# Where SBUF buffers start: weights on multiples of 2048 bytes, TensorE's activations and the other large buffers 256 bytes past one, on one Trainium2 core

## The chip, the core and the metric

The kernel runs on one core of a Trainium2 chip. Its time is the device time of one execution in microseconds (us); each version is run several times, and the median counts. The engines are TensorE (PE), VectorE (DVE), ScalarE (ACT), GpSimd (POOL) and SyncE (SP), which issues the transfers. A profiled execution of the kernel before gives the trace that is read below.

## The reference

One transformer-like layer in fp32 over B=4 sequences of T=2048 tokens with D=512 channels, modulated by a small matrix (`wmod`):

```python
mod = (silu(c) @ wmod).reshape(4, 6, 1, -1)
sa, ca, ga, sb, cb, gb = (mod[:, i] for i in range(6))
# ga and gb keep their sign and are at least 0.25 in size
h = layernorm(x) * (1 + ca) + sa
x = x + ga * attn(h)
h = layernorm(x) * (1 + cb) + sb
x = x + gb * ffn(h)

# attn: per token omega, zeta and B from h (three projections, 256 columns in all), a scan over
# time of a 2 x 64 state, then xs @ C.T + h @ D_mat.T
# ffn: xr, xk are mixes of a token with the one before it;
#      sigmoid(xr @ Wr.T) * (square(relu(xk @ Wk.T)) @ Wv.T)
```

## The kernel before

Work goes by *chunks* of 512 tokens (16, index q) for the first norm, the projections and the scan, and by *units* of 256 tokens (32, index u) for the rest. P=128 partitions, KC=4 slices of the 512 channels. Every engine has its own instruction stream, written out by hand as a loop over the units; semaphores (`s_...`) tie them together. Nothing else sets the order.

Each matrix product is made in three passes from a high and a low half in fp32r (`_hi`, `_lo`): hi*hi, hi*lo and lo*hi, four slices each. `product()` issues them as `pe.matmul(out, act[a][k], weight[w][k])`. The second argument is loaded into the array (the *stationary* tile, an LDWEIGHTS of 128 columns, 512 bytes a partition), the third streams through it (*moving*). One load goes with each matmul. In every unit PE does:

- `k_product`: `wk` stationary, `mix_k` (256 columns) moving, 48 matmuls into `ps_kr`
- `t2_blocks`: 8 transposes with `xn2` stationary and `ident` moving
- `cd_product`: 24 matmuls with `h` stationary and a row of `wd` (512 columns, 2048 bytes) moving, then `states_part`, 6 with `xs` stationary and `wc` moving, into `ps_cd`
- `r_product`: 24 with `mix_r` stationary and `wr` moving, 512 columns, into `ps_kr`
- `v_product`: 24 with `kk` stationary and `wv` moving, 512 columns, into `ps_tv`
- in every second unit `projections`, 24 with `proj` stationary and `h` moving, 512 columns, and 16 transposes of `x_in` (stationary)

All of these but the transposes carry line 328 (`product`) in the trace, so they are told apart by their tiles, out<-in.

Buffers are placed one behind the other in the order of their declaration by `sb(...)`, from byte 1152 of each partition on. So a buffer's address follows from the sizes of those ahead of it. The remainders of the start address, in bytes (every slice that is used adds a multiple of 512):

| buffer | role on PE | past a multiple of 2048, before | past a multiple of 128, before | past a multiple of 2048, after |
|---|---|---|---|---|
| `proj`, `wk` | stationary | 1152 | 0 | 0 |
| `wd`, `wc`, `wr`, `wv` | moving | 1152 | 0 | 0 |
| `h` (both pairs) | stationary, moving in the projections | 384 | 0 | 256 |
| `mix_k` | moving | 576 | 64 | 256 |
| `mix_r`, `kk_hi`, `kk_lo` | stationary | 576 | 64 | 256 |
| `xs_hi`, `xs_lo` | stationary | 2016 | 96 | 256 |
| `xn2` | stationary | 576 | 64 | 256 |
| `x_in` | stationary | 1728 | 64 | 256 |
| `ident` | moving | 1152 | 0 | 256 |
| `x2`, `h_full` | none | 384 | 0 | 256 |
| `rt`, `kk`, `mix_full` | none | 576 | 64 | 256 |
| `xs` | none | 2016 | 96 | 256 |
| `gate_a`, `gate_b` | none | 1696 | 32 | 256 |
| `square_out1` | none | 352 | 96 | 256 |
| `om_pos`, `ze`, `ee` | none | 576 | 64 | 1728 |

Before, the buffers end at byte 229344; after, at 228428.

The second norm (LN2) of a unit runs over several engines: DVE multiplies the product in `ps_cd` by the gate into `xn2` (`rt` for unit 1) and adds it to `x2` with a sum; ACT makes the mean and then, in `statistics2`, the squares with their sum; POOL makes the reciprocal root; DVE writes the normalised unit into `xn2` (`normalise2`), which PE transposes. ACT's squares are wanted for their sums alone; where the squares themselves go, nobody reads.

Of the kernel before, what the change touches and what calls it, by code (L numbers as in the profile page):

```python
# [7 lines left out]
F32 = mybir.dt.float32  # L8
F32R = mybir.dt.float32r
# [3 lines left out]
B, T, D, M = 4, 2048, 512, 64  # L13
P = 128
# [24 lines left out]
def build(nc, d):  # L39
    ctx = ExitStack()  # L40
    with ctx:
# [5 lines left out]


        proj = [sb(f"proj_{n}", [P, KC, 256], F32R) for n in ("hi", "lo")]
        wd = [sb(f"wd_{n}", [P, KC, D], F32R) for n in ("hi", "lo")]  # L50
        wc = [sb(f"wc_{n}", [P, D], F32R) for n in ("hi", "lo")]
        wk = [sb(f"wk_{n}", [P, KC, D], F32R) for n in ("hi", "lo")]
        wr = [sb(f"wr_{n}", [P, KC, D], F32R) for n in ("hi", "lo")]
        wv = [sb(f"wv_{n}", [P, KC, D], F32R) for n in ("hi", "lo")]
        ident = sb("ident", [P, P])
        scan_bias = sb("scan_bias", [P, 4])
# [10 lines left out]
        cur_m = sb("cur_m", [P, NTAB])  # L67
        gate_a = sb("gate_a", [P, D])
        gate_b = sb("gate_b", [P, D])
        minus_half = sb("minus_half", [P, TPC])  # L70

        x_in = sb("x_in", [P, TPC, D])
        gate_cols = sb("gate_cols", [P, 3, 2, B * D // P])
# [6 lines left out]
        bn = sb("bn", [P, TPC, 2])  # L80
        square_out1 = sb("square_out1", [P, 2, D], mybir.dt.bfloat16)
        square_out2 = sb("square_out2", [P, 2, D], mybir.dt.bfloat16)
        rstd1 = sb("rstd1", [P, TPC])
        h_full = sb("h_full", [P, KC, CHUNK])
        h = [[sb(f"h_{n}{i}", [P, KC, CHUNK], F32R) for n in ("hi", "lo")] for i in range(2)]

        x2 = sb("x2", [P, 4, TPU, D])
        sum2 = sb("sum2", [P, 2, TPU])
# [4 lines left out]
        last_n = sb("last_n", [P, KC])  # L93
        mix_full = sb("mix_full", [P, 2, KC, UNIT])
        mix = [mix_full[:, n] for n in range(2)]


        with nc.sbuf_tensor("stage_mix", [P, 2, KC, D], F32) as stage_mix:
            pass
        mixs = [[sb(f"mix_{n}_{w}", [P, KC, UNIT], F32R) for w in ("hi", "lo")] for n in "kr"]  # L100
        with nc.sbuf_tensor("stage_kk", [P, KC, D], F32) as stage_kk:
            pass
        kks = [sb(f"kk_{m}", [P, KC, UNIT], F32R) for m in ("hi", "lo")]
        with nc.sbuf_tensor("stage_out", [P, KC, D], F32) as stage_out:
            pass
        xn2 = sb("xn2", [P, TPU, D])
        rt = sb("rt", [P, TPU, D])
        kk = sb("kk", [P, 2, 2 * UNIT])

        om_pos = sb("om_pos", [P, HALF])  # L110
# [9 lines left out]
        state = sb("state", [P, 3, HALF + 1])  # L120
        xs = sb("xs", [P, CHUNK])
        xss = [sb(f"xs_{m}", [P, CHUNK], F32R) for m in ("hi", "lo")]

# [444 lines left out]
        def _(act):  # L568
# [8 lines left out]
            def squares(x, neg_mean, scratch, out, count, s_sq):  # L577

                for i in range(out.shape[1]):
                    if count + i >= 2:  # L580
                        act.wait_ge(s_sq, count + i - 1)
                    act.activation(scratch[:, i % 2, :], x[:, i, :], ACT.Square, bias=neg_mean[:, i:i + 1],  # L582
                                   accum_out=out[:, i:i + 1]).then_inc(s_sq, 1)
# [5 lines left out]
            def statistics2(u):  # L589
                act.wait_ge(s_x2, u * TPU + TPU)  # L590
                act.activation(neg_mean2[:, u % 2, :], sum2[:, u % 2, :], ACT.Identity, scale=-1.0 / D)\
                   .then_inc(s_mean2, 1)
                act.wait_ge(s_mean2, u + 1)
                squares(x2[:, u % 4], neg_mean2[:, u % 2], square_out2, sq2[:, u % 2], u * TPU, s_sq2)

# [959 lines left out]
```

## Time and profile before

| | |
|---|---|
| median of 3 timed runs | 976.72 us (976.17 to 977.73) |
| the profiled execution, its time | 977.14 us |
| its span in the trace, first to last instruction | 975.4 us |
| busy: PE, DVE, ACT, POOL | 935.9, 820.9, 691.5, 93.5 us |
| mean granted TensorE clock | 0.981 |

A group's "mean ns of one" is the length of one record. Matmuls overlap in it, so the pace of PE is read from the starts: the start of one group of a timeline minus the start of an earlier one, divided by the matmuls between. The granted clock is a share of 2.4 GHz; 0.50 is 1.2 GHz.

### The profile page before, as it was taken

Reading aid. Unit: us, or ns where it says so; the run is one execution under the profiler, and the core shown is the slowest. Engines: PE = TensorE matmul, PEld = TensorE weight load, DVE = VectorE, ACT = ScalarE, POOL = GpSimd, SP = SyncE. Lnnn points to the kernel's source line nnn. Section 1 sums busy time; section 2 is a strip of 40 time slices with the busy share of each in tenths; the row PEclk is TensorE's granted clock in tenths of the full one; section 3 lists DMA queues with packets and bytes.
Section 4 is the critical chain, followed back from the end, with each engine's and each line's share of the span. In section 5 each row is a group of like instructions: output and inputs, shape, how many; then the busy total and the mean of one; then the engine's idle time right before and its main releaser. Section 6 shows DMA issues by size and latency. Waiting matters only on the chain.

```text
span 975.4 us, 14746 instructions
## 1 busy us (share of the span) xinstructions
PE 935.9 (96%) x5012; PEld 786.9 (81%) x5012; DVE 820.9 (84%) x2280; ACT 691.5 (71%) x1354; POOL 93.5 (10%) x117
## 2 busy tenths in 40 slices
PE   9995979899999999999999999999999999998997
PEld 3574858788888888888888888888888888887886
DVE  4897779898989989898998979898997989697562
ACT  4979765768777686777868686877768677765451
POOL 0001010001100202010200101110110201000000
PEclk9997998999999999999999999999999999999999
DMA  9820311020211312021121312021131201111001
GB/s 327 280 56 23 109 34 53 12 98 23 87 55 44 99 44 70 18 87 44 57 85 44 98 32 77 23 87 45 44 98 44 98 6 39 44 44 44 23 22 44
DMA packets 35275, 64.78 MB, mean 66 GB/s; under 512 B 3704, under 2 KB 4344, under 8 KB 35200
## 3 DMA queue, kind: packets, MB, share of 16 engines
q1 hardware_dynamic: 35200, 63.84, 19.8%
q8 instruction: 40, 0.66, 0.3%
q14 instruction: 35, 0.29, 0.1%
HBM read 47.02 MB, written 16.81 MB: 65 GB/s over the span
## 4 chain that ended last, share of the span: by engine, by line
PE 83%; DVE 8%; ACT 6%; issue 1%; DMA 1%; DVEq 0%; SPq 0%; ACTq 0%
PE ps_kr L328 32%; PE ps_cd L328 20%; PE ps_tv L328 18%; PE ps_pt L328 7%; PE ps_tv L369 3%; PE ps_pt L336 3%; ACT mix_full L734 1%; DMA stage_out<-in_wd 1%; DVE mix_full L985 1%; PE ps_cd L376 1%; DVE tmp L1206 1%; ACT x_in L600 1%; DVE state L1210 1%; PE ps_tv L389 0%; DVE tmp L1130 0%
## 5 line engine op out<-in xcount | busy, mean ns | idle before, releaser
L985 DVE SCALAR_TENSOR_TENSOR mix_full<-ps_tv,cur_m,mix_full 128x256 f32<-128x256 f32 x256 | 119.1, 479 | 37.7 <-ACT mix_full L734 37.6
L756 ACT ACTIVATE kk<-ps_kr 128x512 f32<-128x512 f32 x64 | 38.1, 599 | 123.4 <-PE ps_kr L328 123.1
L734 ACT ACTIVATE mix_full<-ps_tv,cur_m 128x255 f32<-128x255 f32 x256 | 120.0, 573 | 1.8 <-PE ps_tv L369 1.8
L1484 POOL TENSOR_SCALAR var<-sq 128x2 f32<-128x2 f32 (+1 forms) x34 | 37.1, 1091 | 642.5 <-ACT square_out L582 642.5
L328 PE MATMUL ps_kr<-mix_k_hi,wk_hi 128*128 128x256 f32 x512 | 80.9, 281 | 8.2 <-issue 8.2
L328 PEld LDWEIGHTS ps_kr<-mix_k_hi,wk_hi 128*128 128x128 f32 x512 | 71.2, 191 | 11.2 <-issue 8.8
L328 PE MATMUL ps_kr<-mix_k_hi,wk_lo 128*128 128x256 f32 x512 | 80.1, 279 | 0.0
L328 PE MATMUL ps_kr<-mix_k_lo,wk_hi 128*128 128x256 f32 x512 | 80.0, 279 | 0.0
L328 PE MATMUL ps_kr<-wr_hi,mix_r_hi 128*128 128x512 f32 x256 | 71.5, 402 | 5.5 <-ACT kk L756 5.5
L328 PE MATMUL ps_tv<-wv_hi,kk_hi 128*128 128x512 f32 x256 | 72.8, 408 | 0.8 <-issue 0.8
L328 PE MATMUL ps_kr<-wr_hi,mix_r_lo 128*128 128x512 f32 x256 | 69.9, 395 | 0.0
L328 PE MATMUL ps_tv<-wv_lo,kk_hi 128*128 128x512 f32 x256 | 69.9, 395 | 0.0
L328 PE MATMUL ps_kr<-wr_lo,mix_r_hi 128*128 128x512 f32 x256 | 69.8, 395 | 0.0
L328 PE MATMUL ps_tv<-wv_hi,kk_lo 128*128 128x512 f32 x256 | 69.1, 392 | 0.0
L328 PEld LDWEIGHTS ps_kr<-mix_k_lo,wk_hi 128*128 128x128 f32 x512 | 69.0, 190 | 0.0
L328 PEld LDWEIGHTS ps_kr<-mix_k_hi,wk_lo 128*128 128x128 f32 x512 | 68.6, 190 | 0.0
L328 PE MATMUL ps_cd<-wd_hi,h_hi 128*128 128x512 f32 x248 | 68.1, 396 | 0.0
L328 PE MATMUL ps_cd<-wd_lo,h_hi 128*128 128x512 f32 x248 | 66.4, 390 | 0.0
L328 PE MATMUL ps_cd<-wd_hi,h_lo 128*128 128x512 f32 x248 | 66.4, 389 | 0.0
L748 ACT ACTIVATE mix_k_hi<-mix_full 128x512 fp32r<-128x512 f32 x64 | 40.4, 641 | 33.9 <-DVE mix_full L985 33.6
L328 PEld LDWEIGHTS ps_kr<-wr_hi,mix_r_hi 128*128 128x128 f32 x256 | 47.6, 191 | 15.7 <-issue 5.9
L328 PEld LDWEIGHTS ps_tv<-wv_lo,kk_hi 128*128 128x128 f32 x256 | 49.1, 192 | 11.3
(213 smaller groups left out, 2239.6 us busy)
## 6 DMA issues: line engine op xcount, KB each, us to landing
x<-in_x SPq DMA_DIRECT2D x32, 512.0 KB, 3.7
out<-x SPq DMA_DIRECT2D x32, 512.0 KB, 2.8
x_in<-in_x SPq DMA_DIRECT2D x15, 1024.0 KB, 5.1
x<-in_wmod SPq DMA_DIRECT2D x3, 1024.0 KB, 7.6
mix_full<-in_wmod SPq DMA_DIRECT2D x2, 1024.0 KB, 9.1
x_in<-in_x SPq DMA_DIRECT2D x2, 512.0 KB, 5.7
stage_out<-in_wd SPq DMA_DIRECT2D x1, 1024.0 KB, 10.0
stage_mix<-in_wmod SPq DMA_DIRECT2D x1, 1024.0 KB, 10.5
```

Of the source, the lines that this page charges most:

```text
L328: mm = pe.matmul(out, act[a][k], weight[w][k], start=acc0 and a == 0 and w == 0 and k == 0, stop=acc1 and (a, w) == passes[2] and k == n - 1)
L336: mm = pe.transpose(ps_pt[:, k % 2, i * P:(i + 1) * P], x_in[:, i, k * P:(k + 1) * P], ident[:, :])
L369: mm = pe.transpose(ps_tv[:, k // 2, at:at + P], xn2[:, i, k * P:(k + 1) * P], ident[:, :])
L376: pe.matmul(bank, warm[:, 0:P], warm[:, :], start=True, stop=True)
L600: mm = act.activation(x_in[:, i, :], x_in[:, i, :], ACT.Identity, bias=norm_bias1[:, i:i + 1], scale=rstd1[:, i:i + 1])
L734: mm = act.activation(mix[n][:, k, 1:UNIT], ps_tv[:, j, c * UNIT:(c + 1) * UNIT - 1], ACT.Identity, bias=cur_m[:, SHIFT + k:SHIFT + k + 1] ...
L748: act.activation(mixs[n][0][:, 2 * j:2 * j + 2, :], mix[n][:, 2 * j:2 * j + 2, :], ACT.Identity)\
L756: act.activation(kk[:, i, :], ps_kr[:, i, :], ACT.Relu).then_inc(s_relu, 1)
L985: dve.scalar_tensor_tensor(mix[n][:, k, :], ps_tv[:, j, c * UNIT:(c + 1) * UNIT], cur_m[:, alpha + k:alpha + k + 1], mix[n][:, k, :], ALU. ...
L1206: dve.tensor_tensor(t, node, frm.unsqueeze(1).broadcast_to([P, 2, 3, c]), ALU.mult)\
L1210: dve.tensor_reduce(to[:, 0:2], t.rearrange("p i j c -> p i c j"), mybir.AxisListType.X, ALU.add)\
L1484: pool.tensor_scalar(var[:, :], sq[:, :], 1.0 / D, EPS, ALU.mult, ALU.add).then_inc(s_var, 1)
```

## The change

Two unused buffers push the next ones to chosen addresses: `to_2048` (896 bytes) puts `proj` at byte 2048, and since all weights have a multiple of 2048 bytes, the others follow on such multiples; `by_256` (256 bytes) puts everything after it 256 bytes past one. The declarations of the large buffers that are read or written by PE, ACT and DVE come next, all multiples of 2048 bytes long, and the small ones behind them. To make room, `square_out2` is dropped, a bf16 buffer of 2048 bytes for LN2's squares. They now go to `xn2` (to `rt` in unit 1), in fp32, and the two waits of the squares on earlier squares are left out there. No engine's instructions change in number or place.

```diff
+        sb("to_2048", [P, 224])
         proj = [sb(f"proj_{n}", [P, KC, 256], F32R) for n in ("hi", "lo")]
         wd = [sb(f"wd_{n}", [P, KC, D], F32R) for n in ("hi", "lo")]
         wc = [sb(f"wc_{n}", [P, D], F32R) for n in ("hi", "lo")]
         wk = [sb(f"wk_{n}", [P, KC, D], F32R) for n in ("hi", "lo")]
         wr = [sb(f"wr_{n}", [P, KC, D], F32R) for n in ("hi", "lo")]
         wv = [sb(f"wv_{n}", [P, KC, D], F32R) for n in ("hi", "lo")]
+        sb("by_256", [P, 64])
+        h = [[sb(f"h_{n}{i}", [P, KC, CHUNK], F32R) for n in ("hi", "lo")] for i in range(2)]
+        xss = [sb(f"xs_{m}", [P, CHUNK], F32R) for m in ("hi", "lo")]
+
+        with nc.sbuf_tensor("stage_mix", [P, 2, KC, D], F32) as stage_mix:
+            pass
+        mixs = [[sb(f"mix_{n}_{w}", [P, KC, UNIT], F32R) for w in ("hi", "lo")] for n in "kr"]
+        with nc.sbuf_tensor("stage_kk", [P, KC, D], F32) as stage_kk:
+            pass
+        kks = [sb(f"kk_{m}", [P, KC, UNIT], F32R) for m in ("hi", "lo")]
+        with nc.sbuf_tensor("stage_out", [P, KC, D], F32) as stage_out:
+            pass
+        xn2 = sb("xn2", [P, TPU, D])
+        rt = sb("rt", [P, TPU, D])
+        kk = sb("kk", [P, 2, 2 * UNIT])
+        x_in = sb("x_in", [P, TPC, D])
+        h_full = sb("h_full", [P, KC, CHUNK])
+        x2 = sb("x2", [P, 4, TPU, D])
+        mix_full = sb("mix_full", [P, 2, KC, UNIT])
+        mix = [mix_full[:, n] for n in range(2)]
+        xs = sb("xs", [P, CHUNK])
+        gate_a = sb("gate_a", [P, D])
+        gate_b = sb("gate_b", [P, D])
+        square_out1 = sb("square_out1", [P, 2, D], mybir.dt.bfloat16)
+
         ident = sb("ident", [P, P])
...
-        square_out2 = sb("square_out2", [P, 2, D], mybir.dt.bfloat16)
...
                 for i in range(out.shape[1]):
-                    if count + i >= 2:
+                    if scratch is square_out1 and count + i >= 2:
                         act.wait_ge(s_sq, count + i - 1)
                     act.activation(scratch[:, i % 2, :], x[:, i, :], ACT.Square, bias=neg_mean[:, i:i + 1],
...
-                squares(x2[:, u % 4], neg_mean2[:, u % 2], square_out2, sq2[:, u % 2], u * TPU, s_sq2)
+
+                squares(x2[:, u % 4], neg_mean2[:, u % 2], rt if u == 1 else xn2, sq2[:, u % 2], u * TPU, s_sq2)
```

The lines that the diff takes out elsewhere are the same declarations at their old places.

## Rows read from the trace of the kernel before

**Rows 1.** The page's head: span, busy us of each engine.
```profile
span 975.4 us, 14746 instructions
PE 935.9 (96%) x5012; PEld 786.9 (81%) x5012; DVE 820.9 (84%) x2280; ACT 691.5 (71%) x1354; POOL 93.5 (10%) x117
```

**Rows 2.** Windows: stretch, its length, busy us of each engine (instructions), clock, DMA.
```profile
400.00:600.00 200.00, 200.00 (x1107) 172.87 (x1106) 177.53 (x501) 153.38 (x300) 23.27 (x25) 1.00 0.19 60
600.00:800.00 200.00, 200.00 (x1106) 173.05 (x1105) 179.73 (x504) 149.69 (x296) 23.49 (x26) 1.00 0.17 57
```

**Rows 3.** Waits from 200 to 900 us: us in total, times, longest.
```profile
ACT kk L756 <- PE ps_kr L328: 93.9, 40, 4.9
```

**Rows 4.** Timeline of PE, 446 to 476 us: start us, us, group.
```profile
447.35 1.08 PE L328 MATMUL ps_kr<-wr_lo,mix_r_hi 128*128 128x512 f32 x4
...
451.92 1.07 PE L328 MATMUL ps_cd<-wd_hi,h_hi 128*128 128x512 f32 x4
...
453.74 1.07 PE L328 MATMUL ps_cd<-wd_hi,h_lo 128*128 128x512 f32 x4
...
457.37 0.39 PE L328 MATMUL ps_cd<-wc_hi,xs_hi 128*128 128x512 f32 x1
...
458.77 1.08 PE L328 MATMUL ps_tv<-wv_hi,kk_hi 128*128 128x512 f32 x4
459.69 1.08 PE L328 MATMUL ps_tv<-wv_lo,kk_hi 128*128 128x512 f32 x4
...
464.27 0.64 PE L328 MATMUL ps_kr<-mix_k_hi,wk_hi 128*128 128x256 f32 x4
...
465.66 0.62 PE L328 MATMUL ps_kr<-mix_k_hi,wk_hi 128*128 128x256 f32 x4
...
469.74 1.04 PE L369 MATMUL ps_tv<-ident,xn 128*128 128x128 f32 x8
470.53 1.17 PE L328 MATMUL ps_cd<-wd_hi,h_hi 128*128 128x512 f32 x4
```

**Rows 5.** The same, from 439.9 to 446.6 us.
```profile
442.80 1.07 PE L328 MATMUL ps_pt<-h_hi,proj_lo 128*128 128x512 f32 x4
...
446.43 0.39 PE L328 MATMUL ps_kr<-wr_hi,mix_r_hi 128*128 128x512 f32 x1
```

**Rows 6.** Groups by form: count, busy us, mean ns of one, idle before.
```profile
L328 PE MATMUL ps_kr<-wr_hi,mix_r_lo 128*128 128x512 f32 x256 | 69.9, 395 | 0.0
...
L328 PE MATMUL ps_cd<-wd_hi,h_lo 128*128 128x512 f32 x248 | 66.4, 389 | 0.0
...
L328 PE MATMUL ps_cd<-wc_hi,xs_lo 128*128 128x512 f32 x62 | 25.6, 412 | 0.0
```

**Rows 7.** By tile: count, duration in ns min/median/max, first and last start.
```profile
L582 ACT ACTIVATE square_out<-x,neg_mean x64: 705/717/726, 57.1 to 925.9; 128x512 bf16<-128x512 f32 x64
...
L770 ACT ACTIVATE kk_hi<-kk x64: 617/657/689, 90.7 to 960.2; 128x512 fp32r<-128x512 f32 x64
```

**Rows 8.** Near the end: timeline of PE, and a window's clock.
```profile
900.10 0.77 PE L328 MATMUL ps_cd<-wc_hi,xs_hi 128*128 128x512 f32 x1 [4.24 <-DVE xs_lo L916]
...
909.79 0.64 PE L328 MATMUL ps_kr<-mix_k_lo,wk_hi 128*128 128x256 f32 x4
...
914.50 0.64 PE L328 MATMUL ps_kr<-mix_k_hi,wk_lo 128*128 128x256 f32 x4
...
898.20:905.00 6.80, 4.90 (x12) 3.87 (x13) 5.61 (x11) 2.96 (x7) 0.00 (x0) 0.50 0.00 0
```

**Rows 9.** The chain's first 30 us; transfers: count, KB, us to landing.
```profile
12.77 9.96 DMA stage_out<-in_wd
...
x<-in_wmod SPq DMA_DIRECT2D x3, 1024.0 KB, 7.6
mix_full<-in_wmod SPq DMA_DIRECT2D x2, 1024.0 KB, 9.1
```

**Rows 10.** Windows 200 to 976 us: PE reading `wr_hi`, then `wc_hi` (counts).
```profile
200.00:976.00 776.00, 121.93 (x464) 0.99 0.17 54
...
200.00:976.00 776.00, 38.08 (x104) 0.99 0.17 54
```

More of the change, by code:

```diff
@@ L67, in build @@
         cur_m = sb("cur_m", [P, NTAB])
-        gate_a = sb("gate_a", [P, D])
-        gate_b = sb("gate_b", [P, D])
         minus_half = sb("minus_half", [P, TPC])
-        x_in = sb("x_in", [P, TPC, D])
         gate_cols = sb("gate_cols", [P, 3, 2, B * D // P])
@@ L80, in build @@
         bn = sb("bn", [P, TPC, 2])
-        square_out1 = sb("square_out1", [P, 2, D], mybir.dt.bfloat16)
-        square_out2 = sb("square_out2", [P, 2, D], mybir.dt.bfloat16)
         rstd1 = sb("rstd1", [P, TPC])
-        h_full = sb("h_full", [P, KC, CHUNK])
-        h = [[sb(f"h_{n}{i}", [P, KC, CHUNK], F32R) for n in ("hi", "lo")] for i in range(2)]
-        x2 = sb("x2", [P, 4, TPU, D])
         sum2 = sb("sum2", [P, 2, TPU])
@@ L93, in build @@
         last_n = sb("last_n", [P, KC])
[L94 to L108, printed above, removed]
         om_pos = sb("om_pos", [P, HALF])
@@ L120, in build @@
         state = sb("state", [P, 3, HALF + 1])
-        xs = sb("xs", [P, CHUNK])
-        xss = [sb(f"xs_{m}", [P, CHUNK], F32R) for m in ("hi", "lo")]
         x2_a, x2_b = (x2[:, i:i + 2].rearrange("p a t n -> p (a t) n") for i in (0, 2))
```

## The prediction

> **What bounds the kernel now.** I read the page's head first: TensorE is busy for 935.9 of 975.4 us [rows 1]. A share says nothing of who waits, so the windows came next: from 400 to 800 us PE is busy for 200.00 of 200 us twice (the stretch from 200 us on reads alike), while VectorE (DVE) has 177.5 of 200 and ScalarE (ACT) 153.4 of 200 [rows 2]. The longest wait that the sums name between other engines and PE is ACT's for PE, 93.9 us [rows 3]. So every nanosecond by which a matmul follows its forerunner sooner is kept, as long as DVE, with a tenth of the time free, does not come into the way. Before 200 us the chain runs through ACT, DVE and a 9.96 us landing of `wd` [rows 9], and near the end PE waits once, for 4.24 us, for `xs_lo` [rows 8].
>
> Then I read how fast PE goes, from the starts of its groups in one unit in the bound stretch [rows 4]. All products with 512 columns have the same shape, and their pace differs:
> - `wd` products (4 matmuls a row): from 453.74 to 457.37 us are 16 matmuls, 226.9 ns each. The projections from 442.80 to 446.43 us [rows 5]: 226.9 ns also.
> - `wr` products: 447.35 to 451.92 us, 20 matmuls, 228.5 ns. `wv`: 459.69 to 464.27 us, 20 matmuls, 229.0 ns. Together 9.15 us for 40, 228.8 ns.
> - `wc` products: 457.37 to 458.77 us, 6 matmuls, 233.3 ns.
> - `wk` products with 256 columns: 465.66 to 469.74 us, 36 matmuls, 113.3 ns. That is half of 226.7.
>
> The grouped rows say the same in another way: the mean of one matmul is 389 ns for `wd_hi,h_lo`, 395 for `wr_hi,mix_r_lo`, 412 for `wc_hi,xs_lo` [rows 6].
>
> What differs between them? Not the PSUM tile: `ps_kr` takes the quick `wk` products and the slow `wr` ones. Not the moving operand: in `wd`, `wr`, `wv` and `wc` products it is a 2048-byte row of a weight, all at the same remainder (1152 past a multiple of 2048). Not the step between the slices of the stationary tile: it is 1024 bytes in the slow `wr` and in the quick projections alike. What is left is where the stationary tile starts (the table of addresses above): `h`, `wk` and `proj` start on a multiple of 128 bytes and are quick; `mix_r` and `kk` start 64 past one and are 1.9 ns slower by these rows; `xs` starts 96 past one (480 past a multiple of 512) and is 6.4 slower. The moving operand's remainder does not seem to matter: `mix_k` moves from 64 past a multiple of 128 and its product is at the quick pace. So I read a toll on the load of a stationary tile that starts off 128 bytes, paid by the matmul beside it. It is an inference from pairs of rows; no row shows one product at two addresses.
>
> **The change part by part.** No instruction moves on PE, DVE, SP or POOL. Afterwards `mix_r`, `kk`, `xs`, `xn2` and `x_in` all start 256 past a multiple of 2048, and the weights on one.
> - *`wr` and `wv` products.* From 200 us on `wr_hi` is read 464 times [rows 10], 16 times a unit: 29 units with 24 `wr` and as many `wv` products, 1392 in all. The toll is 228.8 - 226.9 = 1.9 ns by the rounded starts, or 229.0 - 226.9 = 2.1 by the longer-settled `wv`. I take 2.1: **2.9 us**. Bounds 2.6 and 3.2.
> - *`wc` products.* `wc_hi` is read 104 times from 200 us on [rows 10], 4 times a unit: 26 units with 6 products each. At the `wd` pace they would take 1.36 in place of 1.40 us, 0.04 a unit, 1.0 us. But each group of three begins behind a wait on its queue and the first matmuls after such a place are slow everywhere, so a part stays: I take 0.03 a unit, **0.8 us**. Bounds 0 and 1.0.
> - *Transposes.* `x_in` and `xn2` are stationary at 64 past a multiple of 128. Eight take 0.79 us [rows 4] (469.74 to 470.53). These are short, so the load itself should set their pace; if it loses the same 2.1 ns, 16 a unit in as many units give 0.9 us. No row shows an aligned transpose. Bounds 0 and 0.9; I take **0.9**, since the toll seems to sit in the load.
> - *The start of `wk` products.* The first 12 take 1.39 us (464.27 to 465.66) where 12 at the later pace take 1.36 (12 x 113.3 ns) [rows 4]. They follow the `wv` products' off-128 loads; what follows `wr` products has such a slow start as well. Over 28 such units from 200 us on that is 0.8 us at most, 0 at least; I take **0.3**.
> - *LN2's squares into `xn2` (or `rt`).* The square takes 717 ns (median) with a bf16 output [rows 7]. With an fp32 output on the same phase as its input the nearest row is `kk_hi<-kk`: 657 at the median, 617 at the least, without a bias column [rows 7]. The span of that row is 40 ns and of the square's 21, so I put the change at 60 ns more at most; two squares a unit would then add 0.12 us to ACT, which has 46 of 200 us free [rows 2]. If they got quicker, nothing would be won either, since ACT waits for PE. The two dropped waits on `s_sq2` are for squares of the unit before, done before its statistics begin: 0. `xn2` is idle at that point: the products that it held have been added into `x2`, and the normalisation that fills it waits for these squares through POOL. Cost 0, hidden under PE. Without that cover it would be at most 0.12 us in each of 32 units, 3.8 us.
> - *DVE, POOL and the other buffers.* Their operands move too. DVE has 22 of 200 us free [rows 2], so even 1% on all its work, 1.8 us in 200, stays hidden: 0. It would take 12% before DVE set the pace.
>
> Sum: 2.9 + 0.8 + 0.9 + 0.3 = 4.9 us. The profiled execution took 977.14 us, 0.4 above the median of the timed runs, 976.72; 977.14 - 4.9 = 972.2, and for the median of the runs **971.8 us**.
>
> The trace shows a toll on loads beside a running matmul. The Trainium skill, SBUF — State Buffer, section "Who interferes with whom", says that PE and ACT never wait on anyone, and TensorE: Matmul & The Clock Gate, "Step-by-step: what each phase is for", that the weight load has a read port of its own and takes nothing from the matmul that runs. By them, and by 16-byte lines (every address here is a multiple of 32), addresses would not matter and the sum would be 0: 976.7. The two paces of same-shaped products speak against the strict reading, though a toll inside the load alone is not excluded by it.
>
> **The rivals.**
> - *Nothing changes* (976.7, say 975.5 to 977.5). The difference between `wr`/`wv` and `wd` products would come from something else in their order or data. For it: no row tests one product at two addresses. Against it: three sets at 128 bytes are quick, three off it are slow, over many PSUM tiles and neighbours. Chance 0.15.
> - *Slower: the `wk` products lose their quick pace.* Their operands come at a new pair of remainders, moving at 256 and stationary at 0. PE has a slower pace for them: at 909.79 to 914.50 us 40 take 4.71 us, 117.8 ns against 113.3 [rows 8]. If that became the rule in all 28 units of 48, 1344 x 4.5 = 6.0 us come on top, with the `wr`, `wv` and `wc` gain kept: 976.7 - 3.7 + 6.0 = 979.0. It decides from about 60% of the `wk` products on. Against it: the projections have that difference of remainders (moving 384, stationary 128 and 512-byte steps) and are quick. Chance 0.06.
> - *Much faster: the common pace itself falls.* 512 columns at 2.4 GHz are 213.3 ns, and the best rows have 226.9. If the 13.5 ns were a collision of the two reads that this placing removes, a unit of 27.8 us would lose some 1.4 us, 39 us in all: 938. Against it: the quick pace is the same at three pairs of remainders, and is in proportion to the columns, which one load per matmul would not give. Chance 0.03.
> - *Input transfers get quicker.* The landing of `wd` on the chain takes 9.96 us [rows 9]. A 2048-byte row at 576 past a multiple of 2048 touches nine pieces of 256 bytes, at 256 past it eight; if time went with pieces, that is a ninth, 1.1 us: 970.7. DMA: Bandwidth & Descriptors of the Trainium skill, "How a descriptor splits into AXI transactions", tells of such pieces. Against it: a landing of 1024 KB takes 7.6 us into `x` (384 past) and 9.1 into `mix_full` (576 past) [rows 9], both of them off a multiple of 256, which fits their place in a crowded queue better than a count of pieces. Chance 0.04.
> - *The clock.* After the wait of 4.24 us PE had a granted clock of 0.50 for 6.8 us [rows 8], which costs 3.4 us of work at the full clock. One more such stretch in the first 200 us, where PE has gaps of this length, gives 971.8 + 3.4 = 975.2; one less gives 968.4. Chance 0.06 and 0.04.
>
> **How the numbers follow.** The likeliest case, the sum, has 0.62; its own range is 970.8 (all upper bounds: 3.2 + 1.0 + 0.9 + 0.8 = 5.9) to 974.1 (2.6 alone). With the cases above I give 969.0 to 975.6 for 8 in 10: no change and the slower case fall out above (most of 0.21), 938 below. A measurement of this kernel can tell about 0.2% (2.0 us) from no change. Faster by more takes in the sum's case, the transfers, the fewer half-clock stretch, the lower pace and part of the other clock case: 0.76. Within it 0.16, slower 0.08.
>
> **What would show it.** In the profile after: `wr` and `wv` groups of 20 matmuls at 4.54 us in place of 4.57 and 4.58, and means of one at 389 in place of 395; `wc` six in 1.36 to 1.37 us; eight transposes in 0.77 us in place of 0.79; `wd` and projections unchanged at 226.9. ACT's square between 700 and 780 ns. PE still 200.00 of 200 us busy from 400 to 600. I am wrong if `wr` and `wv` keep 228.8 (addresses don't matter, or another remainder does), if `wk` goes to 117.8, or if PE shows waits for DVE or ACT in 200 to 800 us.

## The result, and the profile after

The changed kernel takes 980.12 us (median of 7 runs, 979.34 to 981.29) beside 977.22 for the kernel before: a ratio of 1.0033 with a 95% interval of 1.0023 to 1.0042. The forecast was 971.8 us and a gain; it is 2.9 us of loss, and the time lies above the forecast's range. In the table of the experiments, three executions far above the others of their kernel (1056.54, 1176.49 and 5347.45 us) are left out of the medians.

The page's head of the kernel after, to be read beside [rows 1]:

```profile
span 978.1 us, 14715 instructions
PE 937.2 (96%) x5012; PEld 792.9 (81%) x5012; DVE 820.4 (84%) x2280; ACT 691.0 (71%) x1354; POOL 92.7 (9%) x117
```

The busy engines have as many instructions as before; the 31 fewer in all are recorded waits of ACT, which the squares no longer make.

The windows of the bound stretch, as in [rows 2], and the wait of ACT for PE from 200 to 900 us, as in [rows 3]:

```profile
400.00:600.00 200.00, 200.00 (x1103) 174.05 (x1102) 177.26 (x499) 152.28 (x299) 23.03 (x25) 1.00 0.17 57
600.00:800.00 200.00, 200.00 (x1094) 173.94 (x1093) 177.97 (x505) 148.50 (x293) 22.64 (x24) 1.00 0.18 61
```

```profile
ACT kk L759 <- PE ps_kr L330: 100.7, 41, 5.0
```

PE is still busy in all 200 of 200 us at the full clock, but starts 1103 and 1094 matmuls where it started 1107 and 1106, and ACT waits longer for it, 100.7 us for 93.9. So no new wait came in: the matmuls themselves follow each other less quickly. The timeline of PE says which (one unit; start, duration, group), beside [rows 4]:

```profile
402.66 0.39 PE L330 MATMUL ps_cd<-wc_hi,xs_hi 128*128 128x512 f32 x1
...
404.02 1.07 PE L330 MATMUL ps_tv<-wv_hi,kk_hi 128*128 128x512 f32 x4
404.92 1.07 PE L330 MATMUL ps_tv<-wv_lo,kk_hi 128*128 128x512 f32 x4
...
409.46 0.64 PE L330 MATMUL ps_kr<-mix_k_hi,wk_hi 128*128 128x256 f32 x4
...
411.37 0.64 PE L330 MATMUL ps_kr<-mix_k_lo,wk_hi 128*128 128x256 f32 x4
...
415.21 1.04 PE L371 MATMUL ps_tv<-ident,xn 128*128 128x128 f32 x8
416.00 1.17 PE L330 MATMUL ps_cd<-wd_hi,h_hi 128*128 128x512 f32 x4
...
424.71 1.07 PE L330 MATMUL ps_kr<-wr_lo,mix_r_hi 128*128 128x512 f32 x4
...
429.25 0.93 PE L338 MATMUL ps_pt<-ident,x_in 128*128 128x128 f32 x7
```

- `wv`: 404.92 to 409.46 us are 20 matmuls in 4.54 us, 227.0 ns each, for 229.0. `wr`: 424.71 to 429.25, 4.54 again, for 4.57. Both as forecast.
- `wc`: 402.66 to 404.02, six in 1.36 us, for 1.40. As forecast, and all its steps are 226 or 227 ns: no slow part is left.
- Transposes: eight in 0.79 us (415.21 to 416.00), as before. Forecast was 0.77.
- `wk`: 411.37 to 415.21 are 32 matmuls in 3.84 us, **120.0 ns each, for 113.3**. So it is in every unit from unit 3 on, and in units 0 and 1.

The grouped rows by form say the same, beside [rows 6] (395 and 412 there):

```profile
L330 PE MATMUL ps_kr<-mix_k_hi,wk_hi 128*128 128x256 f32 x512 | 83.2, 285 | 8.2 <-issue 8.2
...
L330 PE MATMUL ps_kr<-wr_hi,mix_r_lo 128*128 128x512 f32 x256 | 69.0, 391 | 0.0
...
L330 PE MATMUL ps_cd<-wc_hi,xs_lo 128*128 128x512 f32 x62 | 24.7, 398 | 0.0
```

The `wk` group shows 285 where the page of before shows 281: 4 ns more, where the steps from start to start grew by 6.7. A pace is read from starts.

The squares, now into `xn2` (the profile's `xn`) in fp32, beside [rows 7]:

```profile
L584 ACT ACTIVATE xn<-x,neg_mean x62: 706/717/727, 56.5 to 928.5; 128x512 f32<-128x512 f32 x62
```

The median is 717 ns as it was with the bf16 output: the term of 0 was right.

**Where the 2.9 us lie.** The `wk` product of unit 3 and that of unit 31, in before and then in after:

```profile
186.01 0.63 PE L328 MATMUL ps_kr<-mix_k_hi,wk_hi 128*128 128x256 f32 x4
...
952.33 0.63 PE L328 MATMUL ps_kr<-mix_k_hi,wk_hi 128*128 128x256 f32 x4
```

```profile
184.82 0.64 PE L330 MATMUL ps_kr<-mix_k_hi,wk_hi 128*128 128x256 f32 x4
...
955.16 0.64 PE L330 MATMUL ps_kr<-mix_k_hi,wk_hi 128*128 128x256 f32 x4
```

After is 1.2 us ahead at unit 3, and its next 28 units take 770.3 us for 766.3, 4.0 more. Where they go can be counted in the two traces, each product from its first start to the first start of what follows it:

| 28 units, us | before | after | difference |
|---|---|---|---|
| `wk` | 153.4 | 162.0 | +8.6 |
| `wr` | 156.4 | 154.9 | -1.4 |
| `wv` | 156.3 | 154.4 | -1.9 |
| `wc` | 39.1 | 38.1 | -1.0 |
| `wd`, projections, transposes | 261.2 | 261.0 | -0.2 |

The sum is the 4.0 us, and 977.14 + 4.0 - 1.2 = 979.9 is the profiled execution's time of 979.97. `wk` loses 8.6 and not 1344 x 6.7 = 9.0 us, as before has slow first steps in this product (116 to 123 ns for the first five) and two units at 117.8.

### The profile page after: what moved, and what is told of

The parts are those of the page before. It is cut to its first block, busy times and chain, and to the rows that moved or that the text cites. A ratio compares the mean times of both kernels' runs of the same rounds, so it can differ in the third digit from the quotient of the medians.

```text
span 978.1 us, 14715 instructions
## 1 busy us (share of the span) xinstructions
PE 937.2 (96%) x5012; PEld 792.9 (81%) x5012; DVE 820.4 (84%) x2280; ACT 691.0 (71%) x1354; POOL 92.7 (9%) x117
## 4 chain that ended last, share of the span: by engine, by line
PE 83%; DVE 9%; ACT 6%; issue 2%; DMA 1%; SPq 0%; DVEq 0%; ACTq 0%
PE ps_kr L330 32%; PE ps_cd L330 19%; PE ps_tv L330 17%; PE ps_pt L330 8%; PE ps_tv L371 3%; PE ps_pt L338 3%; ACT mix_full L737 1%; DVE mix_full L988 1%; DMA x<-in_wmod 1%; PE ps_tv L391 1%; DVE tmp L1209 1%; ACT x_in L603 1%; DVE state L1213 1%; DVE x L1007 0%; DVE tmp L1133 0%
## 5 line engine op out<-in xcount | busy, mean ns | idle before, releaser
L759 ACT ACTIVATE kk<-ps_kr 128x512 f32<-128x512 f32 x64 | 38.1, 598 | 129.4 <-PE ps_kr L330 129.2
L1487 POOL TENSOR_SCALAR var<-sq 128x2 f32<-128x2 f32 (+1 forms) x34 | 39.8, 1169 | 644.5 <-ACT xn L584 593.8
L330 PE MATMUL ps_kr<-mix_k_hi,wk_hi 128*128 128x256 f32 x512 | 83.2, 285 | 8.2 <-issue 8.2
L330 PE MATMUL ps_kr<-mix_k_lo,wk_hi 128*128 128x256 f32 x512 | 82.7, 284 | 0.0
L330 PE MATMUL ps_kr<-mix_k_hi,wk_lo 128*128 128x256 f32 x512 | 82.7, 284 | 0.0
L330 PEld LDWEIGHTS ps_kr<-mix_k_lo,wk_hi 128*128 128x128 f32 x512 | 71.2, 193 | 0.0
L330 PEld LDWEIGHTS ps_kr<-mix_k_hi,wk_lo 128*128 128x128 f32 x512 | 71.1, 193 | 0.0
L330 PEld LDWEIGHTS ps_kr<-wr_lo,mix_r_hi 128*128 128x128 f32 x256 | 48.6, 190 | 10.3
```

Of the source, the lines that this page charges most:

```text
L330: mm = pe.matmul(out, act[a][k], weight[w][k], start=acc0 and a == 0 and w == 0 and k == 0, stop=acc1 and (a, w) == passes[2] and k == n - 1)
L759: act.activation(kk[:, i, :], ps_kr[:, i, :], ACT.Relu).then_inc(s_relu, 1)
L1487: pool.tensor_scalar(var[:, :], sq[:, :], 1.0 / D, EPS, ALU.mult, ALU.add).then_inc(s_var, 1)
```

## The experiments

Theories as they stood. **Own addresses** (P in the later texts): the pace of a product is set by the start addresses of its own two operands. **Handover** (H): a product has several steady paces, and what runs ahead of it picks one. The first runs were to find which move did it. "Before" is the time of the kernel before on the same chip (for the changed kernel the chip is not on record); the paces are means of start-to-start steps in ns from unit 3 on, without the first nine steps of a product, and that of aligned_acts_old_wk is from aligned_acts_again, the same kernel. Addresses are modulo 2048.

| kernel | `mix_k` / `wk` start | us | before | ratio (95%) | `wk` pace |
|---|---|---|---|---|---|
| before | 576 / 1152 | 977.22 | | | 113.3 (two units 117.8) |
| changed kernel | 256 / 0 | 980.12 | 977.22 | 1.0033 (1.0023 to 1.0042) | 120.0 |
| squares_alone | 576 / 1152 | 976.93 | 976.96 | 0.9998 (0.9989 to 1.0007) | 113.3 |
| wk_pair_alone | 256 / 0 | 985.67 | 976.69 | 1.0085 (1.0071 to 1.0099) | 120.0 |
| mixk_by_64 | 320 / 0 | 977.66 | 976.96 | 1.0006 (0.9997 to 1.0016) | 117.8 |
| wk_by_128 | 256 / 128 | 981.24 | 976.96 | 1.0037 (1.0024 to 1.0050) | 119.9, uneven |
| wk_mixk_mixed | 384, 512 / 0, 128 | 978.42 | 976.96 | one run | 119.1, uneven |
| aligned_acts_old_wk | 576 / 1152 | 977.65 | 976.95 | 1.0011 (1.0001 to 1.0020) | 117.8 |
| mixk_by_32 | 288 / 0 | 976.04 | 976.95 | one run | 116.7 |
| aligned_acts_again | 576 / 1152 | 978.75 | 977.27 | one run | 117.8 |
| mixk_by_96 | 352 / 0 | 980.76 | 977.27 | one run | 120.1, uneven |
| kk_also_by_64 | 320 / 0 | 983.10 | 976.95 | 1.0060 (1.0043 to 1.0077) | 117.8 |
| kklo_also_by_64 | 320 / 0 | 980.00 | 976.95 | 1.0029 (1.0017 to 1.0041) | 117.8 |
| nudge_32_columns | 320 / 0 | 973.45 | 977.27 | one run | 113.3 |
| nudge_128_columns | 320 / 0 | 974.14 | 977.27 | one run | 113.3 |
| nudge_32_timed | 320 / 0 | 974.15 | 977.02 | 0.9970 (0.9959 to 0.9981) | 113.3 |
| nudge_32_after | 256 / 0 | 983.50 | 977.02 | 1.0068 (1.0052 to 1.0083) | 120.0 |
| nudge_32_aligned_acts | 576 / 1152 | 980.49 | 977.02 | one run | 117.8 |
| nudge_32_before | 576 / 1152 | 980.28 | 977.02 | one run | 113.3 (unit 29 117.8) |
| nudge_32_from_unit_2 | 320 / 0 | 974.28 | 976.69 | 0.9972 (0.9961 to 0.9983) | 113.3 |

### One part alone

**squares_alone**: the kernel before, with the squares' new target and nothing else.

```diff
-                    if count + i >= 2:
+                    if scratch is square_out1 and count + i >= 2:
-                squares(x2[:, u % 4], neg_mean2[:, u % 2], square_out2, sq2[:, u % 2], u * TPU, s_sq2)
+                squares(x2[:, u % 4], neg_mean2[:, u % 2], rt if u == 1 else xn2, sq2[:, u % 2], u * TPU, s_sq2)
```

> The kernel before with one part of the change alone: LN2's squares go to xn2 (rt in unit 1) and their two waits are left out; every buffer keeps its old address. If the squares cost nothing, as predicted: 977 us, wk at 113.3 ns, wr and wv at 229. If the loss of the changed kernel came from them (theory D): 980 or more, and wk at 119.9.

No change in the time. The target in fp32 and the missing waits cost nothing, so the loss is one of addresses. But units 0 and 1 are at 117.8 ns here and at 113.3 in before, and units 29 and 31 the other way round, at the same addresses: the table's 113.3 for this pair is not fixed by addresses alone.

**wk_pair_alone**, run last, is the plainest test: all of before, and only the `wk` product's two operands at the changed kernel's starts (`wr` and `wv` move by 1024, and so do `h`, `x_in`, `ident`, `x2`, `h_full` and `mix_full`, which the expectation leaves out; the squares' target goes along to make room).

```diff
+        sb("by_896", [P, 224])
         wk = [sb(f"wk_{n}", [P, KC, D], F32R) for n in ("hi", "lo")]
+        sb("by_128", [P, 32])
+        sb("by_704", [P, 176])
+        mix_k = [sb(f"mix_k_{w}", [P, KC, UNIT], F32R) for w in ("hi", "lo")]
+        sb("by_320", [P, 80])
```

> Before's addresses for everything but the `wk` product: `wk` at 0 and `mix_k` at 256 (mod 2048), as in the changed kernel; `mix_r`, `kk` and `xs` keep their remainders, `proj`, `wd` and `wc` too, and `wr`, `wv` go to 128, the same remainder of 1024. Only the squares' scratch goes to `xn2` besides (which was measured at nothing). That the pair decides: `wk` at 120.0 ns in all units, `wr` and `wv` still at 229.0, `wc` at 233.6; 1344 x 5.8 = 7.8 us more than before from 200 us on at most, less what came back elsewhere in the changed kernel (it lost 3 where the terms said 4): 983 to 985 us, ratio 1.006 to 1.008. If instead the loss needs the other moves (the handover from aligned `wv` products): `wk` stays at 113.3, 977 us, ratio 1.000.

The timeline of PE in this kernel:

```profile
433.01 1.08 PE L332 MATMUL ps_tv<-wv_lo,kk_hi 128*128 128x512 f32 x4
...
437.60 0.64 PE L332 MATMUL ps_kr<-mix_k_hi,wk_hi 128*128 128x256 f32 x4
...
439.51 0.64 PE L332 MATMUL ps_kr<-mix_k_lo,wk_hi 128*128 128x256 f32 x4
...
443.35 1.04 PE L373 MATMUL ps_tv<-ident,xn 128*128 128x128 f32 x8
```

`wk` is at 120.0 ns (32 in 3.84 us) and `wv` still at 229.5 (20 in 4.59). The time is 985.7 us, 9.0 over before (8.3 by the ratio), a little more than was expected. In the two traces the 28 units from unit 3 on take 773.8 us for 766.3: `wk` products 7.8 more, all others together 0.3 less. So the move of this pair is enough for the whole loss.

The changed kernel, whose other products are aligned, is 5.1 us quicker than this one by the ratios (1.0033 and 1.0085) and 6.1 by the medians. That is near the forecast's 4.9, but not all of it is pace: in the traces its unit 31 begins 4.9 us sooner (955.2 for 960.0), 1.4 of them by unit 3 (184.8 for 186.2) and 3.4 in the 28 units.

### Other pairs

**mixk_by_64**, the changed kernel with `mix_k` 64 bytes on; `mix_r`, `kk` and what follows go to 512.

```diff
-        mixs = [[sb(f"mix_{n}_{w}", [P, KC, UNIT], F32R) for w in ("hi", "lo")] for n in "kr"]
+        sb("by_64", [P, 16])
+        mix_k = [sb(f"mix_k_{w}", [P, KC, UNIT], F32R) for w in ("hi", "lo")]
+        sb("by_192", [P, 48])
+        mixs = [mix_k, [sb(f"mix_r_{w}", [P, KC, UNIT], F32R) for w in ("hi", "lo")]]
```

> The changed kernel with mix_k alone 64 bytes further (320 past a multiple of 2048; mix_r, kk, xn2 and what follows then stand 512 past one). In the changed kernel a wk matmul follows its forerunner after 119.9 ns, before after 113.3. Theory A, the toll goes by the difference of the two operands' starts (a multiple of 256 is bad): wk back at 113.3, so 1536 x 6.5 ns = 10 us less than the changed kernel, 970 us. Theory B, a moving operand on a multiple of 256 is bad: the same, 970. Theory C, a stationary operand on a multiple of 256 is bad in this product: wk stays at 119.9, time 980. Theory D, the wk pace is not by address at all (squares, other buffers): 119.9, 980. In all of them wr and wv should stay at 226.7 ns, since 512 is a multiple of 128; if they need 256 exactly, they leave it.

**wk_by_128**: the changed kernel with `wk` behind the other weights, 128 bytes on.

```diff
+        sb("by_128", [P, 32])
+        wk = [sb(f"wk_{n}", [P, KC, D], F32R) for n in ("hi", "lo")]
```

> The changed kernel with wk alone on 128 past a multiple of 256 (moved behind the other weights), mix_k still on 256. Theory A (difference a multiple of 256 is bad): 113.3 ns and 970 us. Theory B (moving operand on a multiple of 256 is bad): 119.9 ns and 980 us. Theory C (stationary on a multiple of 256 is bad): 113.3 ns, 970. Theory E (difference a multiple of 128 is bad): 119.9, 980. All others as in the changed kernel.

**wk_mixk_mixed**: halves at different starts, `wk_lo` 128 bytes on, `mix_k_hi` at 384, `mix_k_lo` at 512.

> Three pairs in one kernel, read from the trace alone: mix_k_hi moves from 384 past a multiple of 2048, mix_k_lo from 512, wk_hi is at 0 and wk_lo at 128. Theory A (difference a multiple of 256): hi,wk_hi 113.3, hi,wk_lo 119.9, lo,wk_hi 119.9. Theory B (moving on a multiple of 256): 113.3, 113.3, 119.9. Theory C (stationary on a multiple of 256): 119.9, 113.3, 119.9. Theory E (difference a multiple of 128): all three 119.9.

Moving `mix_k` by 64 gave 117.8 ns with `wr`, `wv` and `wc` still at 226.7 to 227.1: 977.7 us, the loss gone but not the gain won; none of the four theories had this pace. Moving `wk` by 128 gave 119.9, by steps of about 117, 120 and 123 ns in turn where the changed kernel has 120 each time. The mixed kernel has no steady step: they go from 112 to 131 ns, with a mean of 119.1, in an order that repeats in every unit. So its three passes do not tell three pairs apart, as the run was meant to.

Two more distances, edits as in mixk_by_64 with 32 and 224, then 96 and 160 in place of 64 and 192:

> The changed kernel with mix_k 32 bytes further (288 past a multiple of 2048) in place of 64. Theory P knows another pair of addresses here and expects another steady pace than 113.3, 117.8 or 120.0, or one of them by chance. Theory H: entered from the steady wv rhythm, wk settles at the slowest state that this pair allows: over 113.3.

> The changed kernel with mix_k 96 bytes further (352 past a multiple of 2048). Known so far with the quick wv product ahead: 256 past gives 120.0 ns, 288 gives 116.7, 320 gives 117.8. If the rhythms go by the pair, this one has its own, anywhere from 113.3 to 120.

116.7 and 120.1 ns, the latter by uneven steps of 115 to 125. These three kernels (32, 64, 96) differ by the start of `mix_k` alone, with every other buffer at the same address (they ran on three chips), so the moving operand's start matters, in steps finer than 64 bytes, and in no order that I can name.

### The same pair, two paces

**aligned_acts_old_wk**: before's addresses with the `wk` pair kept, and `mix_r`, `kk`, `xn2` at 640, `xs` at 128 (the squares' target moved as well).

```diff
+        mix_k = [sb(f"mix_k_{w}", [P, KC, UNIT], F32R) for w in ("hi", "lo")]
+        sb("by_64", [P, 16])
+        mixs = [mix_k, [sb(f"mix_r_{w}", [P, KC, UNIT], F32R) for w in ("hi", "lo")]]
...
+        sb("by_96", [P, 24])
         xss = [sb(f"xs_{m}", [P, CHUNK], F32R) for m in ("hi", "lo")]
```

> The kernel before, its weights, h, mix_k and x_in at their old addresses, so the wk product keeps its old pair (moving 576, stationary 1152 past a multiple of 2048). New are only mix_r and kk (640 past, a multiple of 128, before 576) and xs_hi and xs_lo (128 past, before 2016), and LN2's squares go to xn2. Theory P, the wk pace goes by the addresses of its own two operands: wk stays at 113.3 ns, wr and wv go from 229.0 to 226.7, wc gets quicker: 972 to 973 us. Theory H, the wk product keeps the state in which the wv product hands over, and the quick steady wv rhythm of 226.7 hands over badly (in the trace before, the two wk products at 117.8 are those whose last wv interval was 227 and not 229 to 231): wk goes to 117.8 in nearly all units, +6.9 us, and with 4.5 us won on the others 978 to 979.

> The kernel of aligned_acts_old_wk once more, for a trace at the full clock; it was timed at 978.1 us, 1.1 above the kernel before, where theory P (own operands alone) gave 972 to 973 and theory H (handover) 978 to 979. Theory H: wk at 117.8 ns in the units that follow a wv product of 226.7, wr and wv at 226.7. If wk is at 113.3 and the time went elsewhere, H falls too.

aligned_acts_again is the same kernel, for a trace at the full clock. Its timeline:

```profile
435.12 0.63 PE L330 MATMUL ps_kr<-mix_k_hi,wk_hi 128*128 128x256 f32 x4
435.59 0.63 PE L330 MATMUL ps_kr<-mix_k_lo,wk_hi 128*128 128x256 f32 x4
...
440.30 0.64 PE L330 MATMUL ps_kr<-mix_k_hi,wk_lo 128*128 128x256 f32 x4
```

From 435.59 to 440.30 us are 40 matmuls, 117.8 ns each, at the very pair of addresses that gives 113.3 in before. Only units 0 and 1, which follow a wait, were at 113.3. So "own addresses" falls as a full account: what runs ahead has a say. It also reads [rows 8] anew: before has both paces at one pair.

How the `wv` product ends can be read beside it. Five traces at the full clock have this pair (before, squares_alone, nudge_32_before, aligned_acts_again, nudge_32_aligned_acts; the nudge is told below), each with 29 `wk` products from unit 3 on. The step from the last `wv` start to the first start after it is 225 to 228 ns ahead of 61 of them, and all 61 go at 117.8; it is 230 to 236 ns ahead of the other 84, and all 84 go at 113.3. Before has both in one trace, 227 ns ahead of units 29 and 31 and 230 to 236 ahead of the other 27, so here neither an address nor the chip can be the difference. In the aligned kernel, with or without the nudge, the step is 225 to 228 in every one of these units, and all are at 117.8. That this last step, or what it stands for, picks the pace is likely at this pair; no run changed it alone.

Do the uneven steps of the `wv` product just ahead (226, 229 and 232 in before, all alike in the aligned kernels) bring the quick pace at another pair too? Two kernels gave `kk` (stationary in `wv`) or `kk_lo` alone the old remainder of 64 again, with `mix_k` at 320 (the diff is that for both halves):

```diff
+        sb("by_64_more", [P, 16])
         kks = [sb(f"kk_{m}", [P, KC, UNIT], F32R) for m in ("hi", "lo")]
+        sb("by_64_again", [P, 16])
```

> mixk_by_64 (mix_k at 320, wk at 0; there the wk product ran at 117.8 ns) with kk as well 64 past a multiple of 128, so that wv goes back to its uneven 226, 229, 232 rhythm while wr and wc stay quick. Theory P: wk stays at 117.8, wv 229.0: 979 us. Theory H: wk goes back to 113.3 ns in nearly all units, wv at 229.0: 977.0 - 1.7 (wr) - 1.0 (wc) = 974.3 us.

> As kk_also_by_64, but kk_lo alone is 64 past a multiple of 128, the stationary tile of the last four of each twelve wv matmuls. Theory P: wk 117.8 ns, 978 us. Theory H: eight of the 24 wv matmuls are uneven, among them the last four, and whether the handover is good depends on where these four leave the rhythm: wk at 113.3 in all or in none; if in all, 973.5 us, the best yet.

Both missed. PE in the first of them:

```profile
432.25 1.10 PE L335 MATMUL ps_tv<-wv_lo,kk_hi 128*128 128x512 f32 x4
...
436.92 0.63 PE L335 MATMUL ps_kr<-mix_k_hi,wk_hi 128*128 128x256 f32 x4
```

`wv` went to 233.5 ns (20 in 4.67 us), not 229.0, and `wk` stayed at 117.8. At 320/0 an uneven forerunner isn't enough: steps of 229 to 236 ns ahead of `wk` go with 117.8 here as 226 and 227 do in mixk_by_64. But the rhythm of before was not brought back either (the steps are 231 and 236 in turn, in kklo_also_by_64 226 to 236), so the test is weaker than it was meant to be. And the stationary start alone doesn't set the toll: `kk` 64 past a multiple of 128 costs 2.3 ns beside a `wv` at 1152, as much beside one at 128 (wk_pair_alone), and 6.7 beside one at 0. It is a matter of pairs there too.

### Changing only the entry

**nudge_32_columns** leaves every address of mixk_by_64 and adds one matmul of 32 columns, the nudge, at the head of each `wk` product. The product's first matmul overwrites its output.

```diff
+                pe.matmul(ps_kr[:, 0, 0:32], wk[0][:, 0, 0:P], mixs[0][0][:, 0, 0:32], start=True, stop=True)
                 for m in range(KC):
```

> mixk_by_64 with one matmul more at the head of each wk product (the same first weight tile and 32 columns of mix_k_hi, into ps_kr, overwritten at once), so all addresses stay and only the entry into the wk product shifts. Theory P: wk stays at 117.8 ns, and the 32 extra loads cost up to 3.5 us. Theory H: wk leaves 117.8 for 113.3 in all units, or, if this shift is an unlucky one, in none; 32 units x 48 x 4.4 ns = 6.8 us gained for at most 3.5 spent.

> The same with 128 columns in place of 32. Theory P: 117.8 ns as in mixk_by_64. Theory H: another shift of the entry, so another chance of 113.3; 117.8 in both nudged kernels would speak against H.

> The kernel of the run with one extra matmul of 32 columns at the head of each `wk` product (`mix_k` at 320, weights at 0), timed against before; its one look gave 973.45 us beside 977.27. Theory H (the `wk` product has several steady paces at one pair of addresses, and what runs ahead of it picks one): the pick repeats from run to run, so 973 to 974.5 us, a ratio of 0.996 to 0.997, faster than both kernels. Theory P (the pace goes by the addresses of the two reads alone; the one look was a chance): 977.7 us as without the extra matmul, or runs that scatter between 973 and 978.

PE in mixk_by_64, and then in nudge_32_timed:

```profile
433.89 0.64 PE L333 MATMUL ps_kr<-mix_k_hi,wk_hi 128*128 128x256 f32 x4
434.36 0.63 PE L333 MATMUL ps_kr<-mix_k_lo,wk_hi 128*128 128x256 f32 x4
...
439.07 0.63 PE L333 MATMUL ps_kr<-mix_k_hi,wk_lo 128*128 128x256 f32 x4
```

```profile
433.18 0.18 PE L473 MATMUL ps_kr<-mix_k_hi,wk_hi 128*128 128x32 f32 x1
433.20 0.70 PE L333 MATMUL ps_kr<-mix_k_hi,wk_hi 128*128 128x256 f32 x4
433.74 0.62 PE L333 MATMUL ps_kr<-mix_k_lo,wk_hi 128*128 128x256 f32 x4
...
438.28 0.62 PE L333 MATMUL ps_kr<-mix_k_hi,wk_lo 128*128 128x256 f32 x4
```

434.36 to 439.07 are 40 in 4.71 us, 117.8 ns; 433.74 to 438.28 are 40 in 4.54, 113.5. The extra matmul costs 0.09 us (0.56 from its start to the second group, for 0.47), 2.9 in 32 units, and 4.5 x 1344 = 6.0 come back: 3.1 net, and 977.66 to 974.15 is 3.5. The time held over six runs, 0.997 of before, quicker than both kernels of the change.

The same nudge in three other kernels:

> The changed kernel itself with the same extra matmul of 32 columns at the head of each `wk` product; addresses as in the changed kernel (`mix_k` at 256, `wk` at 0). H with a further condition, that the pair of addresses decides which paces exist and at 256/0 only 120.0 does: `wk` stays at 120.0 ns, 980 us, ratio 1.003. H alone, where any pair has the quick pace and the entry picks it: 113.3 ns in the units that now have 120.0, 1536 x 6.7 = 10.3 us less the 0.5 us or so that the extra matmuls take, 970 to 971 us. P: 120.0 ns, 980.5 us.

> Before's addresses for the `wk` product (`mix_k` 576, `wk` 1152), the other activations aligned, which gave 117.8 ns for `wk` and 978.1 us, and the extra matmul of 32 columns at its head. H: the extra matmul flips the pick here as well: 113.3 ns from unit 2 or 3 on, 972 to 974 us. P: 117.8 ns stays, 978 us or a little more.

> The kernel before, with the extra matmul of 32 columns at the head of each `wk` product. H: the pick may turn the other way, from 113.3 to 117.8 ns, which would make 1344 x 4.5 = 6.0 us, 983 us; or it stays at 113.3 in all units, the two that had 117.8 included, 976.5 to 977.5. P: 113.3 stays, 977.5 us.

At 256/0 `wk` stays at 120.0, and the kernel only pays for the nudge (3.4 us). At 576/1152 it stays at what it was in either kernel, 117.8 and 113.3, and pays 2.8 and 3.3 us (one run each, against the medians of the kernels without it). H in the form "any pair has the quick pace" falls, and its forecast of 972 to 974 us for the aligned kernel missed by 6.5 or more: an entry can pick a pace, this nudge doesn't pick it everywhere.

**nudge_32_from_unit_2** has the extra matmul under `if u >= 2`:

> The quickest kernel so far (`mix_k` at 320, an extra matmul of 32 columns at the head of each `wk` product, 974.2 us), with the extra matmul only from unit 2 on, since the units 0 and 1 were at 113.3 ns without it and at 117.8 with it. H: 113.3 ns in units 0 and 1 and in all from unit 2 or 3 on. The first 150 us are bound by other things, so this brings 0.4 us at most: 973.6 to 974.2 us, ratio 0.996 to 0.997. P has no reason for a change in units 0 and 1, and expects the same time.

The time is that of nudge_32_timed within the scatter. The forecast on units 0 and 1 failed: unit 0 in mixk_by_64, then in this kernel,

```profile
68.36 0.62 PE L333 MATMUL ps_kr<-mix_k_lo,wk_hi 128*128 128x256 f32 x4
...
72.89 0.62 PE L333 MATMUL ps_kr<-mix_k_hi,wk_lo 128*128 128x256 f32 x4
```

```profile
68.41 0.63 PE L333 MATMUL ps_kr<-mix_k_lo,wk_hi 128*128 128x256 f32 x4
...
73.12 0.63 PE L333 MATMUL ps_kr<-mix_k_hi,wk_lo 128*128 128x256 f32 x4
```

40 matmuls take 4.53 us in the one and 4.71 in the other, 113.3 and 117.8 ns, though both programs have the same instructions at the same addresses up to there. What differs is the moment of entry behind a wait, or the chip: the two ran on different ones. In units 0 and 1 the pace differs in the same way between before and squares_alone. That leaves a hole in the reading of the nudge as well. All kernels at 320/0 without it from unit 2 on (three, on two chips) had 117.8 there and all with it (four, on three other chips) 113.3, but none of each ran on the same chip. Against a property of the chip: aligned_acts_again and nudge_32_aligned_acts had 117.8 at their pair on two of the three chips where the nudged 320/0 had 113.3; without the nudge, units 0 and 1 at 320/0 were at 113.3 on one chip and 117.8 on the other, and from unit 3 on both were at 117.8; and the kernel before kept its time within 0.6 us beside all of these runs. It is likely the nudge; it isn't shown.

## Why the prediction was wrong

Point by point, by its own steps:

- **`wr` and `wv`, 2.9 us; `wc`, 0.8.** Right in direction and nearly in size: in the steady part of a unit 226.7 ns for 229.0 and 233.6, and in the 28 units 3.3 and 1.0 us, where the upper bounds were 3.2 and 1.0. The rule behind it, a toll on a stationary start off 128 bytes whatever it runs beside, is too simple: with `kk` at 576 it was 2.3 or 6.7 ns by where `wv` stood. The part of `wc` that was to stay slow behind its waits did not: no wait stands there in the bound stretch.
- **Squares, 0.** Right: 717 ns for 717, and squares_alone at 0.9998.
- **Transposes, 0.9.** Wrong, 0: eight still take 0.79 us. The bound of 0 was the right end.
- **The start of `wk` products, 0.3.** The slow start is gone (the first 12 take 1.43 us, 409.46 to 410.89, and 12 x 120.0 is 1.44), but it was a slow start against 113.3 ns, and this pace is gone with it.
- **DVE, POOL, clock.** Nothing in the bound stretch: PE has 200.00 of 200 us.
- **The rival "input transfers get quicker"**, chance 0.04, came true beside the loss. After, beside the 9.96 and 9.1 us of [rows 9]:

```profile
mix_full<-in_wmod SPq DMA_DIRECT2D x2, 1024.0 KB, 7.9
stage_out<-in_wd SPq DMA_DIRECT2D x1, 1024.0 KB, 9.3
```

The runs bear it out. In the eleven kernels that have the targets of these transfers (`stage_out`, `x2`, `mix_full`) on multiples of 256 bytes, the landing of `wd` takes 8.5 to 9.3 us and those into `mix_full` 7.9 to 8.1; in the eight others with a trace at the full clock it is 10.0 to 10.3 and 8.8 to 9.1. The first `wk` product begins at 67.8 to 68.3 us in the eleven and at 68.7 to 69.0 in the eight. The argument against it, a crowded queue, does not explain that. All these targets moved together, so it is not shown which counts, nor that all of the 1.2 us at unit 3 come from there.
- **The step that failed** is this sentence: "The moving operand's remainder does not seem to matter: `mix_k` moves from 64 past a multiple of 128 and its product is at the quick pace." From it followed that `wk` would keep 113.3 ns. The sentence generalised from one product at one pair of addresses. mixk_by_64, mixk_by_32 and mixk_by_96 differ from the changed kernel by the start of `mix_k` (and of what lies behind it, whose products kept their pace), and have 117.8, 116.7 and 120.1 ns; wk_pair_alone shows the cost of the pair alone, 9.0 us. In the sum the `wk` products stood with a gain of 0.3 us; they measured a loss of 8.6 in 28 units. The change moved their stationary start too, from 1152 to 0, and no run moves one of the two alone from the pair of before, so how the loss divides between them is open.

What came true was the rival "slower: the `wk` products lose their quick pace", given 0.06. It was priced at 117.8 ns, the only slower pace in the trace of before. With the measured 8.6 us in place of its 6.0 its own sum is 976.7 - 3.7 + 8.6 = 981.6, and with the 1.2 us that the first units won, 980.4, against 980.1. The argument held against it, that the projections have the same difference of remainders and are quick, took a product of 512 columns as evidence for one of 256. In the changed kernel the projections even have the very starts of the `wk` product, moving 256 and stationary 0, and go at 226.7 ns while `wk` goes at 120.0; so a pair of starts has no pace of its own either, apart from the shape that is read. And the 40 matmuls at 117.8 ns in [rows 8] were a warning that was read only as a price: a product with two paces at one pair of addresses can't have its pace from the stationary start alone.

The strict reading of the Trainium skill (SBUF — State Buffer, "Who interferes with whom") in the prediction, that addresses would not matter, made 976.7 us; wk_pair_alone, where they alone move 9 us, disagrees with it.

Open is what makes a pair good or bad, and what picks the pace where there are two: at 576/1152 it went with the last step ahead, at 320/0 with the nudge and not with that step.

## What to carry to other kernels

A pace that some product has now is an asset of its present placing, not a floor: before moving buffers of a kernel that TensorE bounds, list the start-to-start step of every product, and count each one whose operands move, the quick ones above all, as at risk. Move one product's operands at a time; here the good moves (4.5 us in the 28 units) and the bad one (8.6) came in one edit and hid each other. Read paces from starts over 20 or more matmuls, since the mean durations showed 4 of the 6.7 ns. And a product can have two paces at the same addresses, so one trace of it is one sample.

## What the runs showed of the hardware

- A product of 256 columns in fp32r with a weight load beside each matmul had four paces with even steps at the full clock: 113.3, 116.7, 117.8 and 120.0 ns. Which it had went with the starts of its two operands: 256/0 gave 120.0; 288/0, 116.7; 320/0 and 576/1152, 113.3 or 117.8. Two pairs gave uneven steps, 256/128 with a mean of 119.9 and 352/0 with 120.1, and so did the mix of 384 and 512 with 0 and 128, 119.1.
- At 576/1152 the pace went with the last step ahead: 225 to 228 ns and then 117.8 in 61 products, 230 to 236 and then 113.3 in 84, over five traces.
- Products of 512 columns at 256/0 (projections after the change) had 226.7 ns, those of 256 columns at 256/0 120.0.
- With 512 columns the paces were 226.7, 229.0 and 233.4 to 233.6; 229.0 with `kk` at 576 against `wv` at 1152 or 128, the highest with `kk` at 576 against `wv` at 0, and with `xs` at 2016 against `wc` at 1152. At `kk_hi` 512 and `kk_lo` 576 the mean of `wv` was 230.2.
- From about its tenth matmul on a product kept its pace to the end of its 48, in every unit at the full clock. At 320/0 one extra matmul of 0.09 us at its head went along with the change from 117.8 to 113.3 in each of 29 units.
- Eight transposes took 0.79 us at every placing tried.
- Transfers of 1024 KB landed sooner where their targets, moved together, were on multiples of 256 bytes: `wd` in 8.5 to 9.3 us (eleven kernels) for 10.0 to 10.3 (eight).
